# A hybrid block's attention stage: two groups of 64x64 products a turn in place of four, the key scores one turn ahead, the full-size products in two double stretches

## The reference, cut to what matters

```python
q = (x @ W_q).reshape(b, t, H, DK)...      # H, DK, DV = 16, 64, 64
k = (x @ W_k)...; v = (x @ W_v)...
def step(carry, qkv):
    S_K, C_QV, G = carry
    k_C = einsum('bhk,bhkv->bhv', k_t, C_QV)
    G = G + k_t[..., :, None] * k_C[..., None, :]
    S_K = S_K + k_t[..., :, None] * k_t[..., None, :]
    C_QV = C_QV + q_t[..., :, None] * v_t[..., None, :]
    S_C = einsum('bhkj,bhjv->bhkv', S_K, C_QV)
    o_t = einsum('bhk,bhkv->bhv', q_t, S_C - G)
out @ W_o
```

## Time and profile before

| | |
|---|---|
| median of 3 runs | 1033.69 us (1032.54 to 1034.43) |
| the profiled execution's own time | 1031.72 us |
| its span, first to last instruction | 1030.0 us |
| PE busy (matmul) | 1003.6 us, 97% of the span |
| DVE busy | 616.6 us, 60% |
| ACT busy | 491.8 us, 48% |
| granted TensorE clock | 1.00 in the whole span |
| attention's turns | about 241 to 904 us, some 20 us each |

### The profile page before, as it was taken

The page is one execution under the profiler, slowest core; times in us unless marked ns, Lnnn a source line. Parts: engine busy times, 40 slices in busy tenths (PEclk is TensorE's granted clock), DMA queues, the critical chain, the costliest instruction groups (busy, mean ns, idle before and its releaser), DMA issues.

```text
span 1030.0 us, 41963 instructions
## 1 busy us (share of the span) xinstructions
PE 1003.6 (97%) x19166; PEld 906.8 (88%) x19166; DVE 616.6 (60%) x1252; ACT 491.8 (48%) x925; POOL 111.5 (11%) x130
## 2 busy tenths in 40 slices
PE   8999999999999999999999999999999999999998
PEld 6888798999988998899889989998899988889897
DVE  7888877763445544555465554563564457767773
ACT  5676766643343433343444334333443344456663
POOL 2461331220000000000000000000000000113130
PEclk9999999999999999999999999999999999999999
DMA  9422000023324323342234233422343343200101
GB/s 316 154 57 82 1 2 1 1 83 111 119 85 121 110 85 105 105 122 89 85 120 131 86 105 105 126 85 85 105 138 93 106 125 110 80 22 21 42 31 52
DMA packets 60735, 92.75 MB, mean 90 GB/s; under 512 B 7056, under 2 KB 50448, under 8 KB 59536
## 3 DMA queue, kind: packets, MB, share of 16 engines
q1 hardware_dynamic: 60288, 90.07, 28.0%
q10 hardware_dynamic: 272, 0.00, 0.0%
HBM read 48.63 MB, written 41.42 MB: 87 GB/s over the span
## 4 chain that ended last, share of the span: by engine, by line
PE 94%; DVE 2%; ACT 2%; issue 2%; DMA 0%; POOL 0%; SPq 0%; ACTq 0%; DVEq 0%; POOLq 0%
PE bank L223 7%; PE bank L224 6%; PE bank L225 6%; PE bank L1187 6%; PE bank L1213 6%; PE bank L1198 5%; PE bank L1247 4%; PE bank L1235 3%; PE bank L1177 3%; PE bank L1224 3%; PE bank L805 3%; PE bank L807 3%; PE bank L1248 3%; PE bank L1249 3%; PE bank L1263 3%; PE bank L1179 3%
## 5 line engine op out<-in xcount | busy, mean ns | idle before, releaser
L1473 ACT COPY qt<-bank 128x512 f32<-128x512 f32 x64 | 37.6, 587 | 149.3 <-PE bank L225 149.3
L1609 DVE STREAM_TRANSPOSE k<-kt 128x512 f32<-128x512 f32 x64 | 43.4, 697 | 108.8 <-ACT kt L1468 59.0
L1468 ACT COPY kt<-bank 128x512 f32<-128x512 f32 x64 | 37.6, 587 | 116.5 <-PE bank L225 116.5
L1630 DVE TENSOR_TENSOR state_s<-bank,state_s 128x256 f32<-128x256 f32 x124 | 46.7, 419 | 73.5 <-ACT ut L1486 71.5
L1247 PE MATMUL bank<-wo_hi,ot_hi 128*128 128x256 f32 x256 | 74.9, 293 | 0.8 <-issue 0.8
L223 PE MATMUL bank<-ln_xhi,wq_hi 128*128 128x256 f32 x256 | 75.4, 295 | 0.0
L223 PE MATMUL bank<-ln_xhi,wk_hi 128*128 128x256 f32 x256 | 75.2, 294 | 0.0
L1198 PE MATMUL bank<-qt,state_s 64*64 64x64 f32 x2048 | 69.5, 220 | 3.2 <-issue 3.2
L1623 DVE TENSOR_TENSOR state_z<-bank,state_z 128x512 f32<-128x512 f32 x62 | 39.9, 685 | 54.4 <-PE bank L1235 54.3
L1520 ACT ACTIVATE D_hidden<-bank,b_sb 128x512 f32<-128x512 f32 x64 | 44.1, 690 | 59.3 <-PE bank L1264 59.3
L224 PE MATMUL bank<-ln_xlo,wq_hi 128*128 128x256 f32 x256 | 72.4, 283 | 0.1
(11 more groups left out here) (161 smaller groups left out, 2919.3 us busy)
## 6 DMA issues: line engine op xcount, KB each, us to landing
k_rows_scratch<-k SPq DMA_DIRECT2D x32, 512.0 KB, 2.9
k<-k_rows_scratch SPq DMA_DIRECT2D x128, 128.0 KB, 3.5
u_rows_scratch<-sc_and_k SPq DMA_DIRECT2D x31, 512.0 KB, 3.1
landed<-u_rows_scratch SPq DMA_DIRECT2D x124, 128.0 KB, 3.3
out_dram<-xres SPq DMA_DIRECT2D x16, 256.0 KB, 2.1
xres<-in_L_attn_a_x_dram SPq DMA_DIRECT2D x7, 512.0 KB, 9.8
w_nat<-in_L_ffn_W_dram SPq DMA_DIRECT2D x2, 1024.0 KB, 9.6
raw<-in_L_attn_b_W_q_dram SPq DMA_DIRECT2D x1, 1024.0 KB, 12.1
```

## The change

The 64x64 products of a turn now stand in two stretches. The first holds the products by both states, u_and_s and o_by_scores; the second change_z, the key scores of the **next** turn, and the scores of u. The full-size products stand in two double stretches between them (`first_products`, `second_products`). `by_states` is cut into two functions, `by_state_s` and `by_state_z`, since the part with `state_z` has to wait for other semaphores. `kt` gets a second buffer, PSUM banks are dealt out anew, and the programs of ACT, DVE and SyncE follow the new order. The number of matmuls is the same.

```diff
-            kt = place("kt", 40, [P, PAIRS, 2, B, CHUNK])
+            kt_slots = [place(f"kt{n}", kb, [P, PAIRS, 2, B, CHUNK]) for n, kb in enumerate((92, 40))]
...
-            AB, ZB, BB, XB = WB, UB[0], UB[0], (WB[1], WB[0])
+            AB, ZB, BB, XB = UB[0], UB[1], OB, UB[1]
...
-                def by_states(j, b):
+                def by_state_s(j, b):
+
+                    for p in range(PAIRS):
+                        for h in range(2):
+                            last = nc.tensor.matmul(bank[UB[b][p // 4]][half(h), u_cols(p, 0)], state_s[half(h), b, p, :],
+                                                    qt[half(h), j // 2 % 2, p, j % 2, b, :],
+                                                    start=(p % 4 == 0), stop=False, skip_group_check=True)
+                    last.then_inc(by_s_done, 1)
+
+                def by_state_z(j, b):
 
                     for p in range(PAIRS):
                         cols = slice(p * CHUNK, (p + 1) * CHUNK)
                         for h in range(2):
-                            if j < CHUNKS:
...
-                            if j:
-                                last = nc.tensor.matmul(bank[OB[b]][half(1 - h), cols], state_z[half(h), b, p, :],
-                                                        qt[half(h), (j - 1) // 2 % 2, p, (j - 1) % 2, b, :],
-                                                        start=(p == 0), stop=False, skip_group_check=True)
-                    last.then_inc(by_state_done, 1)
+                            last = nc.tensor.matmul(bank[OB[b]][half(1 - h), cols], state_z[half(h), b, p, :],
+                                                    qt[half(h), j // 2 % 2, p, j % 2, b, :],
+                                                    start=(p == 0), stop=False, skip_group_check=True)
+                    last.then_inc(by_z_done, 1)
...
+                def first_group(j):
+
+                    if j < CHUNKS:
+                        pe.wait_ge(a_masked, 2 * (j + 1))
+                        if j:
+                            pe.wait_ge(s_added, 4 * j)
+                        by_state_s(j, 0)
...
+                        by_state_s(j, 1)
+                    if j:
...
+                        pe.wait_ge(b_masked, 2 * j)
+                        for b in range(B):
+                            by_state_z(j - 1, b)
+                    if j < CHUNKS:
+                        pe.wait_ge(by_s_done, 2 * (j + 1))
+                        pe.wait_ge(krow_done, 2 * (j + 1))
+                        u_and_s(j)
+                    if j:
+                        pe.wait_ge(by_z_done, 2 * j)
+                        pe.wait_ge(v_done, 2 * j)
+                        o_by_scores(j - 1)
...
+                def second_group(j):
+
+                    pe.wait_ge(ut_done, 4 * (j + 1))
+                    if j < LAST_STATE:
+                        pe.wait_ge(s_added, 4 * (j + 1))
+                    if j:
+                        pe.wait_ge(urow_done, 2 * j)
+                        change_z(j - 1)
+                    if j + 1 < CHUNKS:
+                        scores_of_keys(j + 1)
+                    if j:
+                        pe.wait_ge(o_low, 2 * j)
+                    scores_of(j, lambda p, h, b: ut[half(h), b, p, :], BB, b_ready)
...
+                def second_products(j):
+
+                    if j:
+                        pe.wait_ge(v_done, 2 * j + 1)
+                        out_product(j - 1)
...
+                    for n, (blk, x) in enumerate(k_parts(j, True)):
+                        if n and j > 0:
+                            pe.wait_ge(x_added, j)
+                        project_k(blk, x)
...
                 for j in range(CHUNKS):
                     first_group(j)
...
+                    first_products(j)
                     if j == CHUNKS - 1:
...
+                    second_group(j)
+                    if j < CHUNKS - 1:
+                        second_products(j)
```

More of the change, by code:

```diff
@@ L1045, in norm_of, with kt_of @@
             def norm_of(j):
-                return (j + 3) // 4 if j % 4 == 1 and j > 4 else None
+                return j // 4 + 1 if j % 4 == 0 and 0 < j <= CHUNKS - 4 else None
+            def kt_of(blk):
+                return kt_slots[blk % 2]
             def prepare_at(t):
@@ L1311, in first_group @@
[L1311 to L1329, removed]
+                        if norm_of(j - 1) == 2 * NBLK:
+                            pe.wait_ge(ln.low_done[0], START + (nd + 1) * DC)
+                        elif norm_of(j - 1):
+                            pe.wait_ge(x_low, 2 * (norm_of(j - 1) - 1))
@@ new lines, in first_products @@
+                def first_products(j):
+                    blk = j // 2 + 1
+                    for n, (blk, x) in enumerate(k_parts(j, False)):
+                        if n == 0:
+                            pe.wait_ge(k_done, 4 * blk + 2)
+                            if j == 0:
+                                pe.wait_ge(v_done, 2)
+                        project_k(blk, x)
+                    for n, (blk, x) in enumerate(q_parts(j, False)):
+                        if blk == LAST_BLOCK:
+                            pe.wait_ge(k_done, 4 * blk + 3 + n)
+                        elif n == 0:
+                            pe.wait_ge(q_done, 4 * blk + 2)
+                        project_q(blk, x)
+                    for n in early_ups(j, False):
+                        pe.wait_ge(gelu_done, n // 2 * 2)
+                        up(n)
+                    if j:
+                        for x in range(2):
+                            if q_parts(j, False):
+                                blk, part = q_parts(j, False)[x]
+                                pe.wait_ge(q_done, 4 * blk + part + 1)
+                            elif k_parts(j, False):
+                                blk, part = k_parts(j, False)[x]
+                                pe.wait_ge(k_done, 4 * blk + part + 1)
+                            elif early_ups(j, False):
+                                pe.wait_ge(gelu_done, early_ups(j, False)[x] + 1)
+                            else:
+                                pe.wait_ge(q_done, 4 * KQ_BLOCKS)
+                            values(j, x)
@@ L1341, in tensor @@
                     project_q(0, x)
+                for x in range(2):
+                    pe.wait_ge(q_done, 2 - x)
+                    project_k(1, x)
+                scores_of_keys(0)
+                for x in range(2):
+                    pe.wait_ge(k_done, 4 + 2 - x)
+                    values(0, x)
                 for j in range(CHUNKS):
-                    even, blk = j % 2 == 0, q_block(j) or k_block(j)
                     first_group(j)
[L1346 to L1407, removed]
-                        elif norm_of(j):
-                            pe.wait_ge(x_normal, 4 * (norm_of(j) - 1))
-                            for k in range(DC):
-                                for c in range(CH):
-                                    last = nc.tensor.transpose(bank[XB[k]][:, c * P:(c + 1) * P],
-                                                               ln.xn[:, c // 2, c % 2, k * P:(k + 1) * P], ident[:, :])
-                                last.then_inc(x_turned, 1)
@@ L1415, in tensor @@
-                    if j < LAST_STATE:
-                        pe.wait_ge(s_added, 4 * (j + 1))
-                    for x in range(2):
-                        if not even:
-                            values(j, x)
-                        elif blk:
-                            project_q(blk, 2 + x)
-                        else:
-                            up(2 + x)
-                    if j == CHUNKS - 1:
-                        ln.pe_transpose(pe, 1, nd, XB)
-                j = CHUNKS
-                first_group(j)
@@ L1440, in tensor @@
+                    second_group(j)
+                    if j < CHUNKS - 1:
+                        second_products(j)
+                pe.wait_ge(v_done, 2 * CHUNKS - 1)
+                out_product(CHUNKS - 2)
+                pe.wait_ge(v_done, 2 * CHUNKS)
+                up(FC)
+                first_group(CHUNKS)
+                pe.wait_ge(x_added, CHUNKS - 1)
+                up(FC + 1)
+                pe.wait_ge(gelu_done, FC + 2)
                 up(FC + 2)
@@ L1529, in hide, with store_parts @@
                         hidden_high(n)
+                def store_parts(j, second):
+                    for blk, x in k_parts(j, second):
+                        store_k(blk, x)
+                    for blk, x in q_parts(j, second):
+                        store_q(blk, x)
+                    hide(*early_ups(j, second))
                 for x in range(4):
```

249 lines of the change are left out of this document (119 added, 130 removed).

## The result

The changed kernel takes 1084.88 us against 1034.06 us on the same chip: a ratio of 1.049, 95% interval 1.047 to 1.052. That is 51 us more, where 44 were forecast. The profiled execution took 1084.19 us, with a span of 1082.5 us, 52.5 above the 1030.0 of before.

A forecast was written before the change was run, and what follows sets the result against it. TensorE, busy 97% of the span, was taken as the bound. Terms 58.3 - 22 + 9 - 0.8 = +44.5 us on the 1030.0 us span gave 1074.5, so a forecast of 1078 us, range 1064 to 1094.

The forecast's parts named there:

- The states' products apart: In by_states, 31 turns: each state's products alone use two of four array tiles, costing twice per matmul; +58 us.
- The two examples that I priced it from: Turn 0's state_s group and the state_z group behind turn 31: 64 matmuls each, alone, in 2.00 and 2.09 us.
- the test I wrote for the first rival: In the changed profile's middle turns, a state_z product starting amid the state_s ones would make the main term wrong.
- the first rival: state_z products run beside state_s ones on the free tiles, so the 58 us vanish: 1020 us, faster; chance 0.06.
- Fewer stretches: Changes between full-size and 64x64 products on TensorE: 66 stretches instead of 129, 0.35 us each; -22 us.
- Pauses: TensorE waiting for its next 256 instructions, mostly in the scores of u: 19 us instead of 10.7, +9 us.
- Eighteen fast blocks: Blocks of 256 TensorE instructions counted to pass in under 2.7 us along the new order, against ten before.
- Waits at the ends: Query-copy wait gets cover, turn 31's 1.55 us goes, a late gelu costs 1.5 us back; -1 us.
- other waits: Middle-turn waits of TensorE for ACT and VectorE stay covered by other products; no cost.
- The thin cover of the wait for `x_added`: Ahead of the second projection part, one part of 1.4 us covers VectorE's addition, holding by about half a microsecond.

The follow-up runs named there:

- three_ends: Changed kernel with alternating states, projection parts between them and u_and_s, query parts, weight load and early up products rescheduled at the ends: 1027.79 us, ratio 0.993.
- four_ends: As three_ends, with the scores of u moved behind the output product, so four stretches a turn: 1018.65 us, ratio 0.986.
- apart: Kernel before, with only the two states' products taken apart and the wait for batch 1's banks put ahead of all products: 1114.91 us, ratio 1.080.
- alternate: Changed kernel, with the products by the two states alternating again inside its first stretch, two stretches a turn: 1048.23 us, ratio 1.014.
- apart_again: As apart, with the wait for batch 1's banks back between the state_s products of batch 0 and batch 1: 1082.47 us, ratio 1.049.

## Why the prediction was right, point by point

**The states' products apart, +58 us:** right in mechanism, 10 too high (its upper bound, 31 x 1.98, is 61 us and not 62). The states' distances grew by 48 us, and the edit alone, in the kernel before, gave 50 us in time. The difference is the seams. The two examples that I priced it from were groups with a full-size product or an all-tile group on each side; in the middle turns `state_z` begins on its free tiles before the last `state_s` products are through, and `u_and_s` before the last `state_z` ones. That also shows the test I wrote for the first rival to be too strict. A `state_z` product did start amid the `state_s` ones, at 505.27, and yet the rival is wrong: of 64 only a handful mix, and the two groups stand one after the other. One rival I did not name and no run tests: one state's neighbouring products also write into one PSUM bank (`UB[b][p // 4]` or `OB[b]`), while in every group that ran at 15 ns four neighbours write into two. So that the tiles and not the banks set the pace is argued, not shown. Against the banks speaks that a full-size product fills 128 partitions of one bank with 256 columns in 0.12 us, while a pair of these products started every 0.058 us (503.912, 503.970 in turn 12) and filled 64 columns.

**Fewer stretches, -22 us:** right. The steps in and out went from 51.2 to 26.6 us. Of these 24.6 some would be ordinary distances elsewhere, and the remainder of the balance gives 19. The pair `three_ends` and `four_ends` gives it by itself: without distances over 0.42 us and what the low clock cost, 31 stretches make 9.9 us, 0.32 each, where I took 0.35.

**Pauses, +9 us:** right in place, too low in size, and right in number partly by luck. Eighteen fast blocks were counted beforehand and eighteen pauses came, eleven of them in the scores as said. But in the trace, with blocks counted from one remainder of 193 to the next, 20 between 245 and 965 us pass in under 2.7 us: 13 of them end in a pause and seven don't, and the other five pauses stand behind slower blocks. Their total was 24.0 us, not 19. The step that was off is the price: I took the mean of the old ones, 1.07 us, though the new ones mostly lie in blocks that pass whole inside a dense stretch, which the old order hardly had; nine of the eleven distances there are 1.7 to 3.0 us. Cut out of the second stretch they went, and moving the count moved them. That they are the engine waiting for its next block of instructions was my reading of the remainder of 256, and the trace of DMA packets bears it out better than I had seen. The 151 packets of the instruction queue `q8` have 16,384 bytes each; TensorE's own instructions are 38735 before and 38720 after, 256.5 and 256.4 a packet. (The prediction divided the instructions of all engines, which gave 278.) Here is one pause:

```profile
540.60 0.92 PE L1201 MATMUL bank<-qt,ut 64*64 64x64 f32 x49
543.43 0.46 PE L1201 MATMUL bank<-qt,ut 64*64 64x64 f32 x15 [1.92 <-issue]
```

A packet of that queue ran from 541.02 to 541.99, and the engine went on 1.4 us after its end. All eighteen pauses of the changed kernel end 1.2 to 1.6 us after such a packet's end, and all ten of the kernel before 1.2 to 1.5 us. The packets also tell the 20 fast blocks apart. Where a pause followed, the packet had started 0.7 to 2.4 us after the block's first instruction; where none did, 0.6 to 1.1 us before it.

**The clock, not in the prediction: +8.5 us, by the estimate above.** It was the one term that was missing. It is a price on the pauses, and so the whole of the pauses, with the clock, came to 22 us more than before and not 9.

**Waits at the ends, -1 us, and other waits, nothing:** right within 1 us. The wait at turn 31's `change_z` went, one of 1.6 us for the masks came in turn 1, where I had not looked, and the gelu at the end cost 0.8. The thin cover of the wait for `x_added` held in all turns; the first `apart` run shows what happens where another wait loses its cover.

So the time fell into the range in part by luck, by terms that erred against each other: 10 too much for the states; 5 too little for the pauses, 8.5 for the clock and 3 for the stretches.

## What to carry to other kernels

Here, products on a part of the array filled it only where neighbours in program order sat on all four tiles (and, in these groups, wrote two banks), so look at which halves each index chooses before taking a loop apart; taking it apart cost 50 us, more than halving the number of changes between full-size and 64x64 products gave. Merging short products into one long dense run can lose more than the changes it saves: here a stretch costs 0.32 us in and out, and 384 small matmuls and weight loads in a row brought pauses of about 2 us with the clock falling behind some. Of each wait that an edit moves, ask what had covered it.

## What the runs showed of the hardware

- One state's 64 matmuls on two tiles start 28 to 33 ns apart in the mean, those on four tiles 15 ns. Where TensorE waited for its own last products with nothing between, the next one started 0.29 us after the last (`alternate`, 520.33 to 520.62); with the slow step behind it I put the wait at 0.35, an estimate.
- In the changed kernel a block of 256 instructions that passed in 1.9 us was followed by 1.5 to 3.0 us without a start in eleven cases of 17. The Trainium skill, in "Runtime: NRT & Kernel Launch", section Instruction fetch mechanics, calls crossing such a boundary mostly hidden; behind most of the changed kernel's 151 packets nothing shows, behind 18 it was not hidden, 24 us in all.
- The clock fell to its lower level for 3.4 us behind pauses of 2.13, 2.15, 2.16, 2.23 and 2.97 us in the changed kernel, and not behind those of 1.99 and 2.10. In other runs it fell once behind 1.76 us (`three_ends`) and did not behind 2.48 (`apart_again`), so the length of the pause alone doesn't decide.
- Why a fast block is not always followed by a pause: in the traces it goes with the moment at which its instruction packet started. In the kernel before, nine of the twelve blocks under 2.7 us ended in a pause, with the packet's start 0.5 to 1.5 us after the block's first instruction; the other three had it 1.2 to 2.6 us before. In `alternate` the trace has 30 such blocks, not the 50 of my count, and 16 of them end in a pause. In `four_ends` it is one of ten, with nine packets started 0.7 to 1.7 us before. A few blocks of 2.6 us in `alternate` and `three_ends` had a packet 0.1 to 0.3 us late and no pause.
- Left open: what makes a packet start early or late. No run varied that alone.
